# Two transformer layers with a mixture of experts: denser output-projection tiles, the causal mask on VectorE, and two set-up stages laid beside other work

## The reference

```python
x = L0_attn_x                                   # 16 x 512 x 256
xn = _layernorm(x)
x = x + attn0(xn) + ffn0(xn)
xn = _layernorm(x)
return x + attn1(xn) + ffn1(xn)

# attn0: 16 query heads on 4 key heads of 64, rotary, causal;
#   scores + polarity_bias + (1 - exp(-gamma*dist)*causal) * NEG, softmax, V, Wo
# ffn0:  y = x + mha(rmsnorm(x));  y + moe(rmsnorm(y))
#   mha: 16 heads of 16, rotary, scores/4, causal, softmax, V, then @ w_o (256x256)
#   moe: 8 experts, top 2 of the router's softmax, the 320 best tokens of each expert,
#        relu(x@w1)@w2 (256 -> 512 -> 256), times the gate, added to the token's row
# attn1: 16 heads of 16, rotary, no mask, softmax, V, then @ w_out.T + b_out
# ffn1:  time-mix of each token with the one before it, then
#        sigmoid(xr@W_r) * (relu(xk@W_k)**2 @ W_v)
```

## Time and profile before

| | us |
|---|---|
| median of 3 executions | 4605.66 |
| lowest, highest | 4598.96, 4607.07 |
| the profiled execution, its own time | 4602.65 |
| span of its instructions | 4600.6 |
| TensorE busy in that span | 4087.8 (89%) |
| VectorE, ScalarE, GpSimd busy | 2917.0, 2588.7, 2637.1 |

### The profile page before, as it was taken

One profiled execution on the slowest core, in us unless ns is written; L12 is line 12 of the kernel. 1 busy time (PEld: TensorE's weight loads), 2 busy tenths in 40 slices (PEclk: granted clock), 3 DMA queues, 4 the chain that ended last, 5 costly groups with the idle time before them and its releaser, 6 DMA issues. The chain is left out here.

```text
span 4600.6 us, 107899 instructions
## 1 busy us (share of the span) xinstructions
PE 4087.8 (89%) x39132; PEld 2718.8 (59%) x39132; DVE 2917.0 (63%) x7620; ACT 2588.7 (56%) x6209; POOL 2637.1 (57%) x4113
## 2 busy tenths in 40 slices
PE   1699999999999999999999999839399999999999
PEld 0366656665665665665666566526266666666666
DVE  3465665666656656656656656561287777777776
ACT  2366565565565565565655655502177767676766
POOL 2386575675675674765865755614454555455552
PEclk9799999999999999999999999959699999999999
DMA  3243243233333332432432433122342333434330
GB/s 87 57 98 75 69 89 72 76 82 76 72 86 72 82 88 60 94 77 63 102 71 69 89 69 75 52 89 39 66 60 48 54 59 49 60 48 60 48 56 21
DMA packets 215516, 317.22 MB, mean 69 GB/s; under 512 B 22288, under 2 KB 162384, under 8 KB 212944
## 3 DMA queue, kind: packets, MB, share of 16 engines
q1 hardware_dynamic: 211024, 305.08, 32.1%
q0 software_dynamic: 3968, 5.25, 0.7%
HBM read 126.66 MB, written 32.59 MB: 35 GB/s over the span
## 5 line engine op out<-in xcount | busy, mean ns | idle before, releaser
L1331 POOL TENSOR_SCALAR l_prob_wo<-l_prob_wo,l_recip_g 128x128 f32<-128x128 f32 (+3 forms) x1024 | 1095.1, 1087 | 241.1 <-DVE l_recip_g L936 240.7
L1822 DVE TENSOR_REDUCE l_neg_max<-l_bank 128x1 f32<-128x512 f32 x1024 | 684.5, 685 | 287.7 <-PE l_bank L1658 285.1
L1950 ACT ACTIVATE l_pts<-l_bank 128x512 f32<-128x512 f32 x1024 | 598.0, 597 | 326.3 <-PE l_bank L1673 316.0
L918 DVE TENSOR_REDUCE l_neg_max<-l_bank 128x1 f32<-128x128 f32 (+3 forms) x1024 | 489.1, 485 | 438.4 <-PE l_bank L614 432.4
L930 DVE CUSTOM_DVE_ANT_0 l_prob_wo<-l_bank,l_bias 128x128 f32<-128x128 f32 (+3 forms) x1024 | 476.9, 485 | 410.8 <-PE l_bank L665 387.2
L1171 ACT ACTIVATE l_prob_wo<-l_prob_wo,l_neg_max_g 128x128 f32<-128x128 f32 (+3 forms) x1024 | 570.8, 559 | 293.7 <-DVE l_neg_max_g L930 291.7
L1163 ACT ACTIVATE l_pts<-l_bank 128x128 f32<-128x128 f32 (+3 forms) x1024 | 437.1, 436 | 475.8 <-PE l_bank L632 458.7
L676 PE MATMUL l_bank<-ident,l_prob_wo 128*128 128x128 f32 x2560 | 431.5, 284 | 68.6 <-POOL l_prob_wo L1331 31.8
L676 PEld LDWEIGHTS l_bank<-ident,l_prob_wo 128*128 128x128 f32 x2560 | 289.1, 142 | 290.4 <-POOL l_prob_wo L1331 152.2
L1658 PE MATMUL l_bank<-l_ks,l_qs 96*128 96x512 bf16 x1024 | 393.1, 384 | 47.2 <-DMA l_ks<-l_parts 26.8
L1673 PEld LDWEIGHTS l_bank<-l_qs,l_ks 128*128 128x128 bf16 x4096 | 303.5, 97 | 192.5 <-ACT l_pts L1950 30.6
(11 more groups left out here) (265 smaller groups left out, 8476.9 us busy)
## 6 DMA issues: line engine op xcount, KB each, us to landing
l_bias<-bias SPq DMA_DIRECT2D x128, 512.0 KB, 4.5
l_qs<-l_parts SPq DMA_DIRECT2D x384, 128.0 KB
l_ks<-l_parts SPq DMA_DIRECT2D x384, 128.0 KB
l_x<-in_x SPq DMA_DIRECT2D x32, 512.0 KB, 5.2
l_kT<-l_bias SPq DMA_DIRECT2D x128, 128.0 KB, 3.3
l_qT<-l_arena SPq DMA_DIRECT2D x128, 128.0 KB, 3.2
l_qT<-l_bias SPq DMA_DIRECT2D x128, 128.0 KB, 3.0
l_prob_wo<-in_Wo SPq DMA_DIRECT2D x16, 1024.0 KB, 4.8
```

Source lines behind the costliest of these rows:

```text
L918: nc.vector.tensor_reduce(neg_max[:, k:k + 1], S[u % 2][:, 0:(at(u)[2] + 1) * P], AX.X, ALU.max, negate=True).then_inc(s.max_ready, 1)
L1331: nc.gpsimd.tensor_scalar(prob[qt][:, i, :], prob[qt][:, i, :], recip_g[:, k:k + 1], None, ALU.mult).then_inc(s.g_scaled, 1)
L1822: nc.vector.tensor_reduce(neg_max[:, n % (2 * UNITS):n % (2 * UNITS) + 1], S[n % SB][:, :], AX.X, ALU.max, negate=True).then_inc(s.max_rea ...
L1950: nc.scalar.activation(pts[:, q % 2, u % H, :, :], TB[u % 2][:, :].rearrange("p (j q) -> p j q", j=NT), ACT.Exp, scale=DS ** -0.5).then_in ...
```

## The change

1. **Output projections of the 16-wide heads, both layers.** `scale_out` writes only the 16 useful rows of each head, into half of a new tile `dense`: groups 0 and 1 share a tile, and groups 2 and 3. `turn_back` runs once for two groups, `w_o` has 2 tiles without zero rows, and `fill_out` sums two products instead of four. `turn_out` now waits for `scale_out` of the group before, not for its `turn_back`.
2. **Causal mask in `row_max` of `layer0`.** The mask matmul of `scores` is gone. `row_max` is now the kind of instruction that `biased_max` is: it reads the bank and a mask tile, adds, writes the sum back into the bank and the row's extreme beside it.
3. **Bias tiles beside frame -1.** The loop over 16 heads leaves the set-up block. It runs at step -1, behind all that VectorE and ScalarE do in frame -1; it has two scratch tiles, so ScalarE can be a head ahead, and ScalarE's queue issues the 8 stores. The first `exponentials` waits until all 16 heads are made; the first rotary product and the first load of a bias tile wait until all are stored. The fills of `w_o` and `outT` are gone from the block.
4. **The set-up of `layer1` beside `experts`.** Its tiles are allocated before `experts`; GpSimd makes the constants behind those of `experts`, SP loads the weights behind those of the experts. To make room, 6 experts' weights are kept instead of 8, and those of experts 6 and 7 are loaded when experts 0 and 1 are done. `layer1` begins with its first `x` load.

```diff
# layer0, set-up block
-                for g in range(PAIRS):
-                    sp.wait_ge(s.setup, BIAS_FROM + 6 * (g + 1))
-                    sp.dma_start(bias_d[g], bias[:, g % 2, :, :]...).then_inc(s.bias_kept, 16)
-                    sp.wait_ge(s.bias_kept, 16 * (g + 1))
-                nc.gpsimd.memset(outT[:, :, :], 0.0)
# TensorE, scores
-                    nc.tensor.matmul(to[:, 0:w], qs[...], ks[...], start=True, stop=False)
-                    nc.tensor.matmul(to[:, w - P:w], ident_b[:, :], mask_b[:, :], start=False, stop=True).then_inc(s.scores_ready, 1)
+                    nc.tensor.matmul(to[:, 0:w], qs[...], ks[...], start=True, stop=True).then_inc(s.scores_ready, 1)
# VectorE
+                def make_bias():
+                    for h in range(HQ):
+                        d = decay[h % 2]
+                        dve.wait_ge(s.decayed, h + 1)
+                        nc.vector.tensor_tensor(d, d, causal01, ALU.mult).then_inc(s.bias_made, 1)
+                        dve.wait_ge(s.bias_made, 3 * h + 1)
+                        nc.vector.tensor_scalar(d, d, -1.0, -NEG * ROOT, ALU.add, ALU.mult).then_inc(s.bias_made, 1)
+                        dve.wait_ge(s.bias_made, 3 * h + 2)
+                        if h > 3:
+                            dve.wait_ge(s.bias_kept[h // 2 % 2], 16 * (h // 4))
+                        nc.vector.scalar_tensor_tensor(bias[:, h // 2 % 2, h % 2, :], ramp_pos, pol[:, h:h + 1], d, ALU.mult, ALU.add).then_inc(s.bias_made, 1)
-                    nc.vector.tensor_reduce(neg_max[:, k:k + 1], S[u % 2][:, 0:(at(u)[2] + 1) * P], AX.X, ALU.max, negate=True).then_inc(s.max_ready, 1)
+                    w = (at(u)[2] + 1) * P
+                    nc.vector.tensor_tensor_reduce(S[u % 2][:, 0:w], S[u % 2][:, 0:w], mask[:, T - w:T], -1.0, 3.0e38, ALU.add, ALU.min,
+                                                   neg_max[:, k:k + 1]).then_inc(s.max_ready, 1)
-                        if r in (35, 51, 67):
-                            turn_back(f, (r - 35) // 16)
-                        if r == 78:
-                            turn_back(f, 3)
+                        if r in (52, 78):
+                            turn_back(f, (r - 52) // 26)
# ScalarE
+                def decays():
+                    def keep(g):
+                        act.wait_ge(s.bias_made, 6 * (g + 1))
+                        nc.scalar.dma_start(bias_d[g], bias[:, g % 2, :, :]...).then_inc(s.bias_kept[g % 2], 16)
+                    for h in range(HQ):
+                        wait(act, s.bias_made, 3 * (h - 1))
+                        nc.scalar.activation(decay[h % 2], ramp_pos, ACT.Exp, scale=gamma[:, h:h + 1]).then_inc(s.decayed, 1)
+                        if h % 2 and h > 1:
+                            keep(h // 2 - 1)
+                    keep(PAIRS - 1)
# GpSimd, scale_out (both layers)
-                    v = blocks[:, :].rearrange("p (n d) -> p n d", d=32)
+                    v = blocks[:, :].rearrange("p (n d) -> p n d", d=32)[:, :, 0:DS]
+                    to = dense[:, :].rearrange("p (n d) -> p n d", d=32)[:, :, DS * (g % 2):DS * (g % 2 + 1)]
# TensorE, fill_out (both layers)
-                    for g in (2 * side, 2 * side + 1):
+                    for half in range(2):
-                        if r in (88, 89, 90, 93):          # layer0; and 96, 97, 98, 101
+                        if r in (88, 90):                  # and 96, 98
-                        if r in (23, 26):  ... side 0      # layer1; and 25, 27, 29, 31, 33, 35
+                        if r in (23, 26):                  # and 29, 33
# experts, SP
-                for e in range(E):
-                    sp.dma_start(w1[:, e, ...]...); sp.dma_start(w2[:, e, ...]...)
+                for e in range(KEPT):                      # KEPT = 6
+                    load_weights(e)
+                sp.dma_start(L.w_o...); sp.dma_start(L.w_qkv...)   # and 8 more of layer1's loads
...
+                    if 0 <= e - 3 < E - KEPT:
+                        sp.wait_ge(y_done, 3 * (e - 3 + 1))
+                        load_weights(KEPT + e - 3)
```

More of the change, by code:

```diff
@@ L951, in rope @@
                     if e == 0:
+                        if m == 0 and b == 0:
+                            for k in range(2):
+                                dve.wait_ge(s.bias_kept[k], 16 * (PAIRS // 2))
                         if m == 0 and b > 0:
@@ L1646, in layer1, with out_at @@
-        nc.all_engine_barrier(sems_to_clear=range(lo, hi))
+        def out_at(b, half):
+            return (2 * b + half) % OUT_RING
         with nc.Block() as block:
```

285 lines of the change are left out of this document (135 added, 150 removed).

## The result

The changed kernel takes 4484.85 us (median of 4 executions, 4474.58 to 4504.27) against 4605.47: ratio 0.975, 95% interval 0.9736 to 0.9764. It is faster, as forecast, but by 121 us where 187.5 were forecast. 4418 was too low by 67 us, and the time lies above the range's end of 4482. The profiled execution is a quick one: 4474.58 us, span 4472.5.

| stretch | before | after | difference | forecast |
|---|---|---|---|---|
| start to the first `row_max` | 142.74 | 107.25 | -35.5 | -38 |
| from there to the last `biased_max` of `layer0` | 2828.4 | 2776.6 | -51.8 | -83 (masks -48, projection -35) |
| from there to the first `row_max` of `layer1` | 355.3 | 345.3 | -10.0 | -20.5 |
| from there to the end | 1274.2 | 1243.4 | -30.8 | -46 |

What follows compares the result with a forecast made beforehand. TensorE was taken to bound both layers, with GpSimd or VectorE nearly full in some stretches. Head -38, masks -48, projections -35 and -46, layer1's set-up -20.5 sum to -187.5, forecasting 4418 us, range 4362 to 4482.

Steps and rivals of the forecast that it cites:

- The masks: Scores of layer0: removing 1024 small matmuls, 61 us of TensorE, gives -48 us, bounds -61 and -25.
- I take 0.8 of it: Scores half of layer0: 0.8 of the 3.8 us a frame that the mask matmuls take comes back as time.
- VectorE 54 of 84: Scores half of layer0: VectorE is busy 54 of 84 us, so TensorE decides there.
- costed at 0: row_max in layer0: changing the instruction kind, with its mask operand and write into PSUM, was taken to cost VectorE 0.
- the bound of a halved rate: row_max in layer0: writing into the PSUM bank being read adds at most 0.42 us at 320 columns; rival's chance 0.04.
- The head: Start to first scores: first x load 48 us earlier, less 10 for stores, gives -38 us, bounds -50 and -25.
- hidden, just: Head: sixteen heads of bias work end 75 us after the first x load, as the stacks land at 74.4.
- `layer0`'s output projection: Wide half of layer0: fewer products in fill_out give 2.2 us a frame, -35 us, bounds -58 and -19.
- idle 1.73 us: Steps 88 to 103 of layer0: GpSimd's idle time there, 1.73 us, was all counted as gain from fewer products.
- `layer1`'s set-up: Between the last scatter and layer1's first x load: only the barrier remains, giving -20.5 us.
- 0, bounds 0 and +8: experts: the set-up work moved there, GpSimd's copies and fills and SP's loads, costs 0, at most 8 us.
- `layer1`'s output projection: Steps 24 to 35 of layer1: fewer products give -2.9 us a batch, -46 us, bounds -59 and -28.

Runs made afterwards that it cites:

- both_masks: The kernel before with row_max as the new kind of instruction and the mask matmul of scores kept as well; 4604.04 us, ratio 1.0002.
- masks_from16: The kernel before with the mask in row_max for units 16 to 63 of a frame only; 4580.73 us, ratio 0.9949.
- ring4_late: The changed kernel with bias tiles in a ring of four pairs and GpSimd's copies for layer1 after the threshold search's rounds; 4476.27 us, ratio 0.9728.
- four_products: The changed kernel with four products a token tile again in layer0's fill_out; 4542.92 us, ratio 0.9865.
- scratch_act: The changed kernel with row_max writing to SBUF from a frame's ninth unit, four bias pairs, and ScalarE instead of GpSimd copying layer1's ones; 4468.21 us, ratio 0.9711.
- dense_only: The kernel before with the dense tiles alone, two products a token tile in both layers, set-up blocks unmoved; 4559.36 us, ratio 0.9903.
- masks_only: The kernel before with the mask in row_max and no mask matmul in scores, nothing else; 4596.31 us, ratio 0.9981.
- hybrid_two: The changed kernel with four bias pairs, ScalarE's copies, two scales in eight on VectorE, old masks in units 0 to 15; 4456.26 us, ratio 0.9669.

## Why the prediction was wrong

**The masks are the step that failed**, with "I take 0.8 of it", -48. At full clock they gave 1.13 us a frame alone, 18 us, and 1.5 us a frame on top of the dense tiles (173.06 to 171.56), 24 us. The share was wrong: taking the matmuls out of `both_masks` gives 1.56 of their 3.84 us, 0.4 and not 0.8. The price of a matmul fits where TensorE sets the pace, 0.40 us for eight in units 16 to 23 against 0.48. But the share was taken from a mean over the half: VectorE 54 of 84 says nothing of units 8 to 15, where it is busy or waiting for the keys' transfers all the time, and which lost 0.76 us. The text had warned of means over a stage, and then stopped at the half. `masks_from16` shows it: masks in 48 of 64 units give one and a half times the gain of masks in all. Even these 48 units give only 1.7 us of their 2.9, since units 32 to 63 give 0.9 of their 1.9; what holds them was not tested. The new kind of `row_max` was costed at 0 and costs 0.37 us a half. It was neither the bound of a halved rate nor one that the accumulator's read explains.

**The head** came out at -35.5 for -38 by two errors that cancel, which is luck: the stores cost the stacks 2.2 us, not 10, and cost VectorE 15.7 us, not 0. The bias work was called "hidden, just", and that sum had left out `make_bias`'s own wait for `bias_kept`, two pair tiles against a store's landing time that the transfers beside it more than doubled. `ring4_late` gave the 11.3 us back.

**`layer0`'s output projection** was right in size: 2.11 us a frame at full clock for 2.2. The reason given was not, so there is luck in it. GpSimd does not stop the gain in the wide half at its idle 1.73 us, as `four_products` shows (2.40 us), and 0.77 us of the gain lies in the scores half, where the sum had none. (Its 4 x 0.91 for `layer1` is 3.64, not 3.66; nothing hangs on it.)

**`layer1`'s set-up** was right at -21.3 in its place; the step "0, bounds 0 and +8" for what it meets in `experts` was mis-sized at 5.4 us, and 4.7 us in the first stacks were not foreseen. `scratch_act` shows the first cause. The second stays open: kernels with `layer1`'s old memory layout have 70.8 to 71.4, `dense_only` 73.8, those with the whole change 75.1 to 76.4.

**`layer1`'s output projection** gave 2.70 us a batch for 2.9, 43 us for 46. Some 8 of these went into gaps of TensorE in which the profile shows no releaser, and by the price of half a us some 5 more into the lower clock level of the first two batches (13.2 us against 2.9).

In the profiled executions the misses add up: `layer0` 31.2, the stretch of `experts` 10.5, `layer1` 15.2, head 2.5: 59.4. The other 7 are the distance of that execution from the median, 10.3 us after and 3 before.

**What stays open.** Why the keys' transfers land half a us later in some kernels than in others with the same scores half. What keeps the masks' gain in units 32 to 63 at half of what the matmuls take. And when the clock falls: the time at the lower level went from 4.3 to 10.0 us a frame between kernels, and no run here was made to find out why.

## What to carry to other kernels

Price what is taken from the busiest engine in stretches of a few steps, each with its own bound, not by a stage's or a half's mean: where another engine is full for 10 us, the gain there is nothing, a dearer instruction on that engine is paid in full, and a transfer that it waits for does not come sooner because the engines do less. Behind work that is moved "beside" other work stand its own waits and the port, queue or engine that it shares with what runs there; walk through every wait in the moved code with the transfer times of the crowded place. Compare two versions at the same granted clock before saying what an edit is worth, and take the price of the lower level from the stretch in which it fell.

## What the runs showed of the hardware that was not expected

- Each us that TensorE spends at the lower clock level costs 0.42 to 0.53 us in the wide halves and in units 16 to 23, but only 0.08 to 0.25 us in units 0 to 7 and 56 to 63. The time spent there differs by up to 6 us a frame between these kernels, so an edit can gain 2.1 us a frame and show 0.4 (`dense_only`).
- TensorE's gaps without a releaser in `layer1` end 2.5 to 3.9 us after a transfer of an instruction queue (q8) has begun, for instance a packet at 3272.49 us of 1.61 us before this matmul of the changed kernel:

```profile
3275.76 1.44 PE L1728 MATMUL l_bank<-l_mixT,next_w_rkv 128*128 128x512 f32 x2 [1.79 <-issue]
```

  Such packets come every 10 us and mostly cost nothing. That TensorE waits for its code there fits, but was not tested. These gaps over 1 us in `layer1` sum to 1.4 to 1.7 us in the kernel before, `masks_only` and `both_masks`, 9.3 in the changed kernel and 20.5 in `hybrid_two`.
- Reading out a row's extreme takes VectorE 142 ns when the instruction ahead of it writes to PSUM, and 83 ns when it writes to SBUF (`scratch_act`, and `biased_max` in every kernel).
